# Moving the low-half subtractions of the wq, wk and wo pieces from GpSimd to VectorE

## The reference

```python
x = x + _L0_cond_ref(x, itok_B_1_198, L0_cond_weights)      # w = weights[idx]; einsum('bct,bcd->bdt', x, w)
x = x + _L1_cond_ref(x, cond_1[:, None, :], Wq, Wk, Wv, Wo)
# _L1_cond_ref, b = 32, s = 128, 1024 wide, 16 heads:
#   q, k, v = x @ W.T, split into heads;  q = q * min(precision, 4)
#   scores = q @ k.T / 8, masked above the diagonal;  attn = softmax(scores)
#   out = attn @ v;  return out @ Wo.T
```

## Time and profile before

| | |
|---|---|
| Median of 3 runs | 1571.79 us |
| Time of the profiled execution | 1572.23 us |
| Its span, first to last instruction | 1570.9 us |
| Granted TensorE clock, mean | 0.999 |
| PE busy | 1560.3 us (99%) |
| DVE busy | 947.0 us (60%) |
| ACT busy | 829.8 us (53%) |
| POOL busy | 907.6 us (58%) |
| The chain that ended last | 96% PE |

### The profile page before, as it was taken

The page is one execution under the profiler, slowest core; times in us unless marked ns, Lnnn a source line. Parts: engine busy times, 40 slices in busy tenths (PEclk is TensorE's granted clock), DMA queues, the critical chain, the costliest instruction groups (busy, mean ns, idle before and its releaser), DMA issues.

```text
span 1570.9 us, 23295 instructions
## 1 busy us (share of the span) xinstructions
PE 1560.3 (99%) x7563; PEld 1311.4 (83%) x7563; DVE 947.0 (60%) x1700; ACT 829.8 (53%) x2349; POOL 907.6 (58%) x926
## 2 busy tenths in 40 slices
PE   9999999999999999999999999999999999999999
PEld 7888888888888888888888888888888887888887
DVE  5844454443366777666676676666666754555553
ACT  6645555543366666666666666666666622222220
POOL 1545645644266677667655666676677553555552
PEclk9999999999999999999999999999999999999999
DMA  9958888855856665665666466656564596444442
GB/s 321 337 209 281 304 283 300 299 212 219 323 161 187 200 202 180 202 184 186 170 231 221 143 169 195 182 177 187 184 177 136 215 358 240 168 161 166 163 163 85
DMA packets 180010, 333.05 MB, mean 212 GB/s; under 512 B 19890, under 2 KB 104114, under 8 KB 172722
## 3 DMA queue, kind: packets, MB, share of 16 engines
q1 hardware_dynamic: 178738, 323.19, 62.6%
q10 hardware_dynamic: 1152, 8.39, 1.3%
HBM read 184.70 MB, written 134.22 MB: 203 GB/s over the span
## 4 chain that ended last, share of the span: by engine, by line
PE 96%; POOL 1%; DMA 1%; DVE 0%; issue 0%; ACT 0%; SPq 0%; ACTq 0%; DVEq 0%; POOLq 0%
PE p_PJ L711 22%; PE p_PJ L712 22%; PE p_PJ L713 22%; PE p_SC L713 6%; PE p_SC L711 6%; PE p_SC L712 6%; PE p_PV L816 4%; PE p_PV L713 1%; PE p_PV L711 1%; PE p_PV L712 1%; PE p_LP L711 1%; PE p_LP L713 1%; PE p_LP L712 1%; PE p_PV L842 1%; PE p_LP L842 1%; DMA out<-t_LATE 1%
## 5 line engine op out<-in xcount | busy, mean ns | idle before, releaser
L712 PE MATMUL p_PJ<-t_XL,t_WH 128*128 128x512 f32 x1008 | 394.1, 391 | 0.0
L711 PE MATMUL p_PJ<-t_XH,t_WH 128*128 128x512 f32 x1008 | 394.1, 391 | 0.0
L713 PE MATMUL p_PJ<-t_XH,t_WL 128*128 128x512 f32 x1008 | 392.1, 389 | 0.0
L1036 ACT ACTIVATE t_PP<-t_PP,t_st 128x128 f32<-128x128 f32 x512 | 199.5, 391 | 176.4 <-DVE t_st L1216 174.9
L1327 POOL TENSOR_TENSOR t_PP<-t_PP,t_st 128x512 f32<-128x512 f32 x128 | 133.4, 1042 | 206.2 <-DVE t_st L1220 206.2
L713 PEld LDWEIGHTS p_PJ<-t_XH,t_WL 128*128 128x128 f32 x1008 | 189.3, 188 | 40.4
L711 PEld LDWEIGHTS p_PJ<-t_XH,t_WH 128*128 128x128 f32 x1008 | 190.0, 188 | 33.8
L712 PEld LDWEIGHTS p_PJ<-t_XL,t_WH 128*128 128x128 f32 x1008 | 190.0, 189 | 32.3
L1234 DVE TENSOR_REDUCE t_AT<-p_PV 64x256 f32<-64x512 f32 x252 | 171.2, 679 | 55.9 <-ACT t_AC L1057 51.9
L1210 DVE SCALAR_TENSOR_TENSOR t_PP<-p_SC,t_beta,t_mask 128x256 f32<-128x256 f32 x256 | 111.6, 478 | 44.8 <-PE p_SC L713 44.8
L1316 POOL TENSOR_TENSOR t_xl<-t_XT,t_xh 128x512 fp32r<-128x512 f32 x56 | 74.0, 1321 | 94.9 <-ACT t_xh L918 94.2
(11 more groups left out here) (255 smaller groups left out, 3656.6 us busy)
## 6 DMA issues: line engine op xcount, KB each, us to landing
t_XH<-xth_scratch SPq DMA_DIRECT2D x56, 512.0 KB, 5.6
t_XL<-xtl_scratch SPq DMA_DIRECT2D x56, 512.0 KB, 6.2
v_scratch<-t_VR SPq DMA_DIRECT2D x64, 256.0 KB, 4.4
xth_scratch<-t_XH SPq DMA_DIRECT2D x16, 1024.0 KB, 4.0
xtl_scratch<-t_XL SPq DMA_DIRECT2D x16, 1024.0 KB, 6.5
t_VX<-v_scratch SPq DMA_DIRECT2D x32, 512.0 KB, 5.8
at_scratch<-t_AT SPq DMA_DIRECT2D x126, 128.0 KB, 2.0
t_XT<-x SPq DMA_DIRECT2D x31, 512.0 KB, 5.3
```

Source lines behind the costliest of these rows:

```text
L711: pe.matmul(bank, lh, rh, start=first, stop=False, skip_group_check=goes_on)
L712: pe.matmul(bank, lh, rl, start=False, stop=False, skip_group_check=goes_on)
L713: return pe.matmul(bank, ll, rh, start=False, stop=last, skip_group_check=goes_on)
L1036: act.activation(PP[:, u, h, :], PP[:, u, h, :], ACT.Exp, bias=st[:, 0, u, h:h + 1], scale=1.0, accum_out=st[:, 1, u, h:h + 1]).then_inc(a ...
```

## The change

The 48 low halves `OL` are written by VectorE, not by GpSimd. They stand one step after ScalarE's `OH` in the tick order, not four. SyncE's stores of `OH` and `OL` stand one step after the split, not five, and the loads of the raw pieces stand 4.5 or 5 steps earlier. The semaphores `pool_p` and `pool_O` are replaced by `dve_p` and `dve_O`.

```diff
-            p_load.put(quiet(1) - 22 + 11 * (m - 16) if m < 18 else quiet(m - 16) + 7, m)
+            p_load.put(quiet(1) - 22 + 11 * (m - 16) if m < 18 else quiet(m - 16) + 2.5, m)
...
-                O_load.put(O_cell(8 * (c - 1) + k) + 7 if c else quiet(17) + 8, (c, place))
+                O_load.put(O_cell(8 * (c - 1) + k) + 2 if c else quiet(17) + 3, (c, place))
...
# VectorE
                 for m in p_split(tick - TICK):
-                    if m >= 16:
-                        continue
                     raw, high, low = qk_piece(m)
                     dve.wait_ge(act_p, m + 1)
                     dve.tensor_tensor(low, raw, high.bitcast(f32), ALU.subtract).then_inc(dve_p, 1)
...
+                for c, k in O_split(tick - TICK):
+                    m = 8 * c + k
+                    dve.wait_ge(act_O, m + 1)
+                    if m:
+                        dve.wait_ge(dve_O, m)
+                    dve.tensor_tensor(OL[:], wo_rows(O_PLACE[k]), OH[:].bitcast(f32), ALU.subtract).then_inc(dve_O, 1)
...
# GpSimd
-                for m in p_split(tick - 4 * TICK):
-                    if m >= 16:
-                        raw, high, low = qk_piece(m)
-                        pool.wait_ge(act_p, m + 1)
-                        pool.tensor_tensor(low, raw, high.bitcast(f32), ALU.subtract).then_inc(pool_p, 1)
-                for c, k in O_split(tick - 4 * TICK):
-                    m = 8 * c + k
-                    pool.wait_ge(act_O, m + 1)
-                    if m:
-                        pool.wait_ge(pool_O, m)
-                    pool.tensor_tensor(OL[:], wo_rows(O_PLACE[k]), OH[:].bitcast(f32), ALU.subtract).then_inc(pool_O, 1)
                 for c, k in O_add(tick):
-                    pool.wait_ge(pool_O, 8 * c + 4)
+                    pool.wait_ge(dve_O, 8 * c + 4)
...
# SyncE
                 for m in p_split(tick - TICK):
-                    if m < 16:
-                        sp_store_qk(m)
-                for m in p_split(tick - 5 * TICK):
-                    if m >= 16:
-                        sp_store_qk(m)
+                    sp_store_qk(m)
...
-                for c, k in O_split(tick - 5 * TICK):
+                for c, k in O_split(tick - TICK):
                     sp_store_wo(c, k)
```

More of the change, by code:

```diff
@@ L200, in cond_attention @@
         pe_P, act_r, dve_g = sem("v_product"), sem("v_first_product"), sem("v_gathered")
-        act_p, dve_p, pool_p, s_p = sem("qk_high"), sem("qk_low"), sem("qk_low_second"), sem("store_qk")
+        act_p, dve_p, s_p = sem("qk_high"), sem("qk_low"), sem("store_qk")
         l_p = [sem(f"load_qk{n}") for n in range(2)]
@@ L227, in cond_attention @@
         pool_T = sem("wo_sum")
-        act_O, pool_O, s_O = sem("wo_high"), sem("wo_low"), sem("store_wo")
+        act_O, dve_O, s_O = sem("wo_high"), sem("wo_low"), sem("store_wo")
         l_O = [sem(f"load_wo{n}") for n in range(8)]
@@ L1440, in sp_load_qk @@
                     sp.wait_ge(s_V[n], 16 * 16)
-            elif 1 < m < 16:
+            elif m not in (1, 17):
                 sp.wait_ge(dve_p, m - 1)
-            elif m > 17:
-                sp.wait_ge(pool_p, m - 17)
             sp.dma_start(qk_piece(m)[0], (wq, wk)[which][d * 128:(d + 1) * 128, half * 512:(half + 1) * 512]).then_inc(l_p[m % 2], 16)
@@ L1451, in sp_store_qk @@
             sp.dma_start(to[0], high.bitcast(f32).rearrange("p (c e) -> p c e", c=NC)).then_inc(s_p, 16)
-            if m < 16:
-                sp.wait_ge(dve_p, m + 1)
-            else:
-                sp.wait_ge(pool_p, m - 15)
+            sp.wait_ge(dve_p, m + 1)
             sp.dma_start(to[1], low.bitcast(f32).rearrange("p (c e) -> p c e", c=NC)).then_inc(s_p, 16)
@@ L1538, in sp_load_y @@
             if y == 0:
-                sp.wait_ge(pool_O, 32)
+                sp.wait_ge(dve_O, 32)
                 sp_wait_at(NG + 1)
@@ L1547, in sp_load_wo_rows @@
             if c == 0 and place == 0:
-                sp.wait_ge(pool_p, 16)
+                sp.wait_ge(dve_p, 32)
             elif c:
-                sp.wait_ge(pool_O, 8 * (c - 1) + (5, 6, 8, 7)[place])
+                sp.wait_ge(dve_O, 8 * (c - 1) + (5, 6, 8, 7)[place])
                 if place in (0, 3):
@@ L1560, in sp_store_wo @@
             sp.dma_start(woh_d[k][:, cols], OH[:].bitcast(f32)).then_inc(s_O, 16)
-            sp.wait_ge(pool_O, m + 1)
+            sp.wait_ge(dve_O, m + 1)
             sp.dma_start(wol_d[k][:, cols], OL[:].bitcast(f32)).then_inc(s_O, 16)
```

## The result

The changed kernel takes 1586.55 us (four runs, 1585.71 to 1587.24), the kernel before 1572.01 (four runs, 1570.49 to 1572.96): a ratio of 1.0093, with a 95% interval of 1.0076 to 1.011. It is 14.5 us slower, and the forecast of no difference (1571.6, with 1575.0 as the upper end) is wrong. The profiled span is 1585.2 us against 1570.9, at the same granted clock of 0.999.

A forecast was written before the change was run, and what follows sets the result against it. PE was taken to bound the kernel, busy 1560.3 of 1570.9 us. From 1572.23 us profiled, 0 + 0 - 0.2 + 0 gave 1572.0, so 1571.6 against the 1571.79 median; range 1569.8 to 1575.0.

The forecast's parts named there:

- the running one finishes, the waiting DVE one comes before POOL's next, and that one pays: At the shared SBUF port: OL waits only for the fourth `t_PS`; the addition `t_AT` pays about 0.46 us.
- 0.94 for OL: OL on VectorE in each of 48 cells takes 0.94 us, within bounds of 0.68 and 1.63, costing PE 0.
- The lock itself: VectorE with two SBUF inputs and GpSimd exclude each other for a whole instruction; `t_PS`, started first, isn't touched.
- Everything after hangs on PE again, so nothing builds up from cell to cell: After masking, which stays at 451.93 with 0.4 us to spare, no lateness carries over; cost 48 x 0.
- Rival 1: OL loses the port twice, also waiting for `t_AT`; masking 0.32 us late, 8.0 us slower, 1579.6; chance 0.09.
- The 0.15: Delay of masking, exponentials, normalisation and `t_PS` absorbed before PE's product with v pays in full: 0.35 - 0.20 us.
- the 0.2 us wait of PE in rows 3: PE's only listed wait in the changed stretch, once, for `t_PS`; taken as the whole gain in reach.
- the gain of 0.2 us in the sum: POOL without OL: the one stall falls elsewhere or is gone, -0.2 us, with +0.4 at the other end.
- The margins of a cell: Room in one cell: 0.15 us for the chain to `t_PS`, 1.61 for `t_KL`, 0.77 at the gather.
- POOL's 61.9 us less: 48 x 1.29 us of OL go from GpSimd, where it ran ahead of no `t_PS`; gain 0.
- rival 3: SyncE's stores ahead of the six moves hold up ACT's read of the probabilities in 16 cells: 1573.2 to 1576.4; chance 0.04.
- with a count near 48: Sign that the forecast is wrong: a row in PE's waits for `t_PS` or `t_KL` with about 48 or 16 counts.

The follow-up runs named there:

- Experiment 3: Changed kernel with GpSimd's addition behind `t_PS` made to wait until OL is done: 1572.39 us, ratio 1.0001 against the kernel before.
- Experiment 6: Changed kernel with OL behind the low half of k on VectorE and done twice, first into an unused PSUM bank: 1575.87 us, ratio 1.0029 to the kernel before.
- experiment 4: Changed kernel with even pieces' OL on VectorE, odd ones on GpSimd, SyncE's stores and loads as before the change: 1575.06 us, ratio 1.0026 to the kernel before.
- experiment 7: Changed kernel with the subtraction OL done twice, first into an unused PSUM bank: 1602.29 us, ratio 1.0195 against the kernel before.
- experiments 1 and 3: The first: changed kernel with SyncE's stores and loads back in their old places, 1585.85 us, ratio 1.0094 to the kernel before; the other: see Experiment 3.
- experiment 8: Separate kernel without attention, only the port contest of gather, OL, `t_PS` or two 128x512 instructions, and addition, released early or late: 321.21 us, one run.
- experiments 9 to 11: Changed kernel with a VectorE filler of 32, 128 or 224 columns ahead of the gather: 1585.36, 1586.29 and 1572.47 us, one run each.
- the 224 columns: Changed kernel with a VectorE filler zeroing 224 columns of the unused bank ahead of the gather: 1572.47 us, one run.
- experiment 5: Changed kernel with OL ahead of the gather on VectorE: 1627.82 us, ratio 1.0355 against the kernel before.

## Why the prediction was wrong

**The step that failed first: "the running one finishes, the waiting DVE one comes before POOL's next, and that one pays".** The text took 0.94 for OL "since rows 9 show DVE going first and rows 8 have this median". That is one sight of an order of precedence, between other instructions (128 x 512, with 0.8 us left to run), made into a rule. The trace of before has 46 places of this kind, outside the attention, in which VectorE, with two SBUF inputs, asked 0.13 to 1.23 us before the end of a GpSimd instruction with another right behind it, and went ahead of that one. But it also has three (at 100.77, 124.45 and 337.57 us) in which VectorE asked 0.04 us before the end and stood behind the next one:

```profile
100.77 1.00 DVE L1169 TENSOR_TENSOR t_SL<-t_XR,t_SH 128x512 fp32r<-128x512 f32 x1
99.52 1.29 POOL L1316 TENSOR_TENSOR t_xl<-t_XT,t_xh 128x512 fp32r<-128x512 f32 x1
100.77 0.46 POOL L1308 TENSOR_TENSOR t_wr<-t_wr,t_ident 128x128 f32<-128x128 f32 x1
```

So the order could be seen to vary before the change. Here GpSimd's queued instruction went first in 48 of 48 cells. Experiment 3 shows that this is the cause: without the queued addition OL takes 0.93, and everything else of the working comes out to 0.04 us. The lock itself is as the prediction had it: OL is either as long as alone (0.67 to 0.70) or ends 0.54 to 0.61 us behind a GpSimd instruction. The Trainium skill's sentence on it (SBUF — State Buffer, "Who interferes with whom": one of them holds the port pair, the other is blocked fully) agrees with these lengths. Its sentence there that issue order decides who is blocked can't be read from recorded starts: in the changed kernel the addition starts 0.33 to 0.35 us after OL in all 48 cells and goes first.

**The second, in the price: "Everything after hangs on PE again, so nothing builds up from cell to cell".** Rival 1 had the very OL that came, ending 1.63 us after it asked, at a chance of 0.09, but priced it at 8.0 us: 0.32 late, 0.15 absorbed, 0.17 x 48 (which is 8.2). The 0.15 was counted in each cell. Masking, maxima, exponentials, reciprocals, normalisation, transposes, gather, OL, `t_KL`, gather and masking again are one ring that runs through VectorE, ACT and GpSimd, and PE's margin is only how late this ring may stand to PE. What a cell can take in is the idle time in the ring: 0.63 + 0.77 us, less the 0.03 between instructions that stays at both places, makes 1.34. OL brings 1.60 + 0.03. So each cell is 1.63 - 1.34 = 0.29 longer, and measured are 0.30. Only the first cell of each of the two stretches has PE's margin to use up: cells 3 and 37 are 0.11 longer, not 0.30. 48 x 0.30 less 2 x 0.19 makes 14.0 us; from the first cell's scores to the last's the changed kernel takes 14.2 us more, and the spans differ by 14.3. Experiment 6, with 1.43 us of work at the free place (0.09 above 1.34, and cells 0.08 to 0.13 longer), and experiment 4, in which a cell with room follows each one without, show the same ring. My expectation of experiment 6 repeated the error.

**A wrong reading behind a right number.** The prediction took the 0.2 us wait of PE in rows 3 for that of the cell in rows 10, at 555 us. It isn't: that wait stands at 1262.23 us, behind the last OL, it is 0.2 in both kernels, and between 440 and 1190 us the waits of PE list nothing at all. The cell in rows 10 did lose 0.20, which its length shows (13.53 against 13.33), so the 0.15 came out right by luck (experiment 7 confirms it), but the gain of 0.2 us in the sum had no ground. Read rightly, the same rows say that PE's waits miss a stall of 0.2 us.

**What held.** The margins of a cell, with OL at 0.93 (experiment 3). POOL's 61.9 us less, worth nothing: no kernel here is faster than before. SyncE's reordering, rival 3, at 0 (experiments 1 and 3). Clock and PE work unchanged.

**A sign that was wrong.** The prediction would have looked for PE's waits "with a count near 48". They show none, and PE is "99% busy" in both kernels. The waits of the weight loads have that count (50 and 46), and cell length and the vanished idle times of VectorE showed it too.

**What stays open.** What decides who is next. In the kernels above VectorE had the port at once when it asked 0.24 us after the fourth `t_PS` began, was behind the next instruction at 0.35 to 0.52, and ahead of it at 0.60. But the contest by itself had VectorE first at asks within that same stretch, and at one and the same ask it waited for the fourth `t_PS` or not, depending on whether the addition was ready early (experiment 8). So the moment of asking alone doesn't decide. In experiments 9 to 11 the addition's own release moved together with OL's asking, since both hang on the end of the gather, so which of the two moments counts can't be told from them. One reading of the 224 columns needs no precedence: OL took 0.69 there, as alone, with 0.12 to 0.13 us of `t_PS` left, and a waiting OL ends 0.55 behind, so by estimate it needs the port only 0.14 us after its recorded start, when `t_PS` was over. No run here separates this from the rest.

## What to carry to other kernels

Before an instruction is put on another engine, look at who holds the port that it needs at the moment when it will ask, and price it at the wait behind two of the other engine's instructions, unless a trace shows that very pair; a place 1.5 us later was free here. Lateness on a ring of engines that comes round each cell is paid by what exceeds the idle time in the whole ring: a margin towards PE then counts once, not in every cell. Only where the ring has idle time left, so that its start is on time again (experiment 7), does the margin come back in each cell. And judge short stalls of PE (0.1 to 0.6 us a cell here) by the length of a repeated stage and by the waits of the weight loads, not by the busy share or the waits of PE.

## What the hardware did that was not expected

- Who is next at the port is not always VectorE: OL 1.60 to 1.63 us behind two instructions of GpSimd (changed kernel, 48 of 48), and in experiment 5 behind one more `t_PS`.
- A recorded start isn't the taking of the port: VectorE had it at once 0.24 us (experiment 7) and up to 0.45 us (experiment 8) after the recorded start of a GpSimd instruction, which then took 1.50 us, or 1.30 to 1.71, instead of 0.73.
- The loser's price is steady. VectorE's 128 x 512 subtraction ends 0.54 to 0.61 us behind the GpSimd instruction it waited for, though it takes 0.67 to 0.70 alone; GpSimd's 128 x 256 addition takes 1.16 to 1.22 instead of 0.73.
- A 0.24 us filler on the busiest helper engine made the changed kernel 14 us faster (1572.47, one run, against 1586.55).
